# Three split operations moved to GpSimd, the first experts' output added in two halves, one expert result per state early in the scan

## The reference

```
h = layernorm(x) * (1 + ca) + sa
x = x + ga * attention(h)              # 8 heads, latent keys and values, causal softmax
h = layernorm(x) * (1 + cb) + sb
x = x + gb * experts0(h)               # 8 experts of 64 hidden units, top 2 of 8, gelu
h = layernorm(x) * (1 + ca1) + sa1
x = x + ga1 * mixer(h)                 # state-space layer, below
h = layernorm(x) * (1 + cb1) + sb1
x = x + gb1 * experts1(h)              # 8 experts of 512 hidden units, top 2 of 8, gelu

mixer: x_in, res = h @ in_w + in_b     # 256 channels each
       xc = silu(conv4(x_in))
       d_raw, B, C = xc @ x_proj_w + x_proj_b      # 16 columns each
       delta = softplus(d_raw @ dt_w + dt_b)
       for each token: state = exp(delta * A) * state + delta * xc * B ; y = sum_n state_n * C_n
       out = ((y + xc * D) * silu(res)) @ out_w + out_b
```

## Time and profile before

| | |
|---|---|
| median of 3 runs | 1304.76 us (1299.76 to 1305.74) |
| the profiled execution | 1305.41 us, span of its instructions 1303.6 us |
| VectorE busy | 1014.4 us, 78% of the span |
| TensorE busy | 1040.4 us, 80% |
| ScalarE busy | 751.6 us, 58% |
| GpSimd busy | 632.4 us, 49% |
| mean granted TensorE clock | 0.909 of full speed |

### The profile page before, as it was taken

How to read it: one execution, slowest core, us unless ns; L and a number is a source line. 1 busy time by engine, 2 the same in 40 slices (tenths; PEclk the granted TensorE clock), 3 DMA queues, 4 the chain that set the end, 5 groups by cost and what they waited for, 6 DMA issues and landing times. The chain is left out here.

```text
span 1303.6 us, 19636 instructions
## 1 busy us (share of the span) xinstructions
PE 1040.4 (80%) x6224; PEld 702.5 (54%) x6224; DVE 1014.4 (78%) x2221; ACT 751.6 (58%) x1483; POOL 632.4 (49%) x446
## 2 busy tenths in 40 slices
PE   5894679887997889887988889878988788877191
PEld 4551136555655556565665555555655565655181
DVE  3766988689788988799888988799888977699301
ACT  2544446478647766577647765576647764575030
POOL 0102952179334963188335952197335942098402
PEclk8896569989998999989998999989998998989596
DMA  5201202262143503261144403271145404061451
GB/s 165 74 9 58 81 0 90 80 219 81 31 153 134 174 25 128 56 240 60 32 152 163 146 29 133 64 234 49 48 136 188 128 23 144 31 232 54 157 164 45
DMA packets 74151, 137.24 MB, mean 105 GB/s; under 512 B 10504, under 2 KB 44344, under 8 KB 73920
## 3 DMA queue, kind: packets, MB, share of 16 engines
q1 hardware_dynamic: 67936, 123.20, 28.5%
q0 software_dynamic: 5392, 12.59, 3.0%
q10 hardware_dynamic: 720, 0.19, 0.1%
HBM read 116.34 MB, written 15.42 MB: 101 GB/s over the span
## 5 line engine op out<-in xcount | busy, mean ns | idle before, releaser
L1692 DVE TENSOR_TENSOR_SCAN probs_T<-bank,probs_T 128x512 f32<-128x512 f32 x256 | 299.4, 1209 | 8.7 <-ACT bank L1245 7.0
L598 POOL TENSOR_TENSOR probs_T<-step_space,probs_T 128x1024 f32<-128x1024 f32 x112 | 263.8, 2361 | 3.1 <-DVE probs_T L1692 3.1
L1245 ACT ACTIVATE bank<-step_space,a_neg 128x512 f32<-128x512 f32 x256 | 169.5, 685 | 69.8 <-DVE probs_T L1692 65.0
L1170 ACT ACTIVATE probs<-bank,row_neg 128x128 f32<-128x128 f32 (+3 forms) x256 | 135.2, 530 | 125.2 <-DVE row_neg L1555 107.8
L880 PE MATMUL bank<-k_pad,q_lat 128*128 128x512 f32 (+3 forms) x512 | 188.0, 454 | 3.1 <-DMA k_pad<-xc 3.1
L1555 DVE TENSOR_REDUCE row_neg<-bank 128x1 f32<-128x128 f32 (+3 forms) x256 | 122.6, 486 | 82.0 <-PE bank L882 79.9
L617 POOL TENSOR_TENSOR step_space<-step_space,probs 128x512 f32<-128x512 f32 x112 | 142.2, 1269 | 44.1 <-DVE probs L1349 43.8
L844 PE MATMUL bank<-probs,w_ident 128*128 128x512 f32 x256 | 154.0, 687 | 8.1 <-DVE probs L1349 8.1
L1349 DVE TENSOR_TENSOR probs<-probs_T,bank 128x1024 f32<-128x1024 f32 x128 | 153.4, 1199 | 5.5 <-PE bank L1030 3.8
L1030 PE MATMUL bank<-split,select 96*128 96x512 bf16 x128 | 55.8, 436 | 111.8 <-DVE probs L1349 85.1
L791 PE MATMUL bank<-expert_w,hidden 128*128 128x128 f32 x960 | 144.3, 298 | 0.0
(11 more groups left out here) (214 smaller groups left out, 1856.8 us busy)
## 6 DMA issues: line engine op xcount, KB each, us to landing
expert_w<-in_experts_dram SPq DMA_DIRECT2D x120, 512.0 KB, 5.1
probs_T<-b_rows_dram SPq DMA_DIRECT2D x64, 512.0 KB, 4.2
slots_in<-slots_dram SPq DMA_DIRECT2D x24, 256.0 KB, 3.3
results_dram<-slots_out SPq DMA_DIRECT2D x24, 256.0 KB, 4.3
k_pad<-xc SPq DMA_DIRECT2D x64, 64.0 KB, 2.0
x_in<-in_x_dram POOLq DMA_DIRECT2D x8, 256.0 KB, 3.3
gate<-gate_rows_dram SPq DMA_DIRECT2D x1, 2048.0 KB, 7.1
out_dram<-x_out POOLq DMA_DIRECT2D x7, 256.0 KB, 3.6
```

Of the source, the lines that this page charges most:

```text
L598: ins = nc.gpsimd.tensor_tensor(inject[:, n % 3, :, :], u[:], row.unsqueeze(1).to_broadcast([P, DH, T]), ALU.mult)
L1170: f(probs_ring[:, n % 4, 0:(i + 1) * P], bank[SCORE_BANK[n % 4]][:, 0:(i + 1) * P], ACT.Exp, bias=row_neg[:, n % 4:n % 4 + 1], accum_out=r ...
L1245: f(decay(k)[:], delta[:, c, :], ACT.Exp, scale=a_neg[:, c, n:n + 1]).then_inc(dec_ok.sem, 1)
L1692: v.tensor_tensor_scan(state[:, n % 2, c, :], decay(DH * n + c)[:], inject[:, n % 3, c, :], 0.0, ALU.mult, ALU.add).then_inc(st_ok.sem, 1)
```

## The change

GpSimd does the low part's three operations in a new function, `split_last`, ahead of its first inject. It starts when VectorE's middle part is done (`split_mid`), and each operation waits for the one before. The output of the small experts goes to two banks, tiles 0 and 1 to bank 6, tiles 2 and 3 to bank 1, so that VectorE adds and takes statistics in two halves; TensorE waits for bank 1's keys to be copied before, and for both halves before it projects the next keys into bank 1. In the tables, block 3's result is moved from state 0 to ahead of the scan, the quad (fill 8) from state 1 to 0, block 5's result from state 1 to 3, and ScalarE copies the quad after decay 4 in place of 6.

```diff
+        EARLY_OUT = (OUT_BANK, 1)
-        out0_mm = signal("out0_mm", 1)
-        out0_add = signal("out0_add", 1)
+        out0_mm = signal("out0_mm", 2)
+        out0_add = signal("out0_add", 2)
+            def split_last(b):
+                low = slice(2 * L, 3 * L)
+                pool.wait_ge(*(gated_weight(b + 1, BIAS) if b < B - 1 else gated_weight(b, OUT)))
+                pool.wait_ge(split_mid.sem, split_mid.at(b, 1))
+                nc.gpsimd.tensor_tensor(part[low, :], proj[low, :], split[low, :], ALU.subtract).then_inc(split_low.sem, 1)
+                pool.wait_ge(split_low.sem, split_low.at(b, 1))
+                nc.gpsimd.tensor_copy(split[low, :], part[low, :]).then_inc(split_low.sem, 1)
+                pool.wait_ge(split_low.sem, split_low.at(b, 2))
+                nc.gpsimd.tensor_tensor(split[low, :], part[low, :], split[low, :], ALU.subtract).then_inc(split_ok.sem, 1)
             def sum_states(b):
+                split_last(b)
+                pool.wait_ge(split_ok.sem, split_ok.at(b, 1))
                 for n in range(2):
...
-                    pool.wait_ge(out0_mm.sem, out0_mm.at(b, 1))
+                    pool.wait_ge(out0_mm.sem, out0_mm.at(b, 2))
                     gate_proj(b + 1)
...
                     for t in range(NT):
-                        ins = mm(bank[OUT_BANK][:, t * P:(t + 1) * P], gated[:, c, t * P:(t + 1) * P],
-                                 gated_proj[:, c, :], start=(c == 0 and t == 0), stop=(c == C0 - 1), skip_group_check=True)
-                    return ins
+                        ins = mm(bank[EARLY_OUT[t // 2]][:, t * P:(t + 1) * P], gated[:, c, t * P:(t + 1) * P],
+                                 gated_proj[:, c, :], start=(c == 0 and t % 2 == 0), stop=(c == C0 - 1),
+                                 skip_group_check=True)
+                        if c == C0 - 1 and t % 2 == 1:
+                            ins.then_inc(out0_mm.sem, 1)
...
+                if ahead:
+                    pe.wait_ge(k_lat.sem, k_lat.at(b + 1, 1))
                 out0(0)
...
                 if ahead:
+                    pe.wait_ge(out0_add.sem, out0_add.at(b, 2))
                     project(b + 1, 3)
...
                 if behind:
-                    pe.wait_ge(out0_add.sem, out0_add.at(b, 1))
+                    pe.wait_ge(out0_add.sem, out0_add.at(b, 2))
                 early(2)
...
-                dve.wait_ge(out0_mm.sem, out0_mm.at(b, 1))
-                tt(x[:], x[:], bank[OUT_BANK][:].rearrange("p (t d) -> p t d", d=P), ALU.add).then_inc(out0_add.sem, 1)
-                dve.wait_ge(out0_add.sem, out0_add.at(b, 1))
-                ln_stats(b, 2, x, link)
+                for half in range(2):
+                    dve.wait_ge(out0_mm.sem, out0_mm.at(b, half + 1))
+                    tiles = slice(2 * half, 2 * half + 2)
+                    source = bank[EARLY_OUT[half]][:, 2 * half * P:(2 * half + 2) * P].rearrange("p (t d) -> p t d", d=P)
+                    tt(x[:, tiles, :], x[:, tiles, :], source, ALU.add).then_inc(out0_add.sem, 1)
+                    dve.wait_ge(out0_add.sem, out0_add.at(b, half + 1))
+                    ins = ln_half_stats(half, x)
+                link(ins)
+                ln_aggregate(link)
...
                 link(cp(split[:], proj[0:3 * BC, :]))
-                mark(tt(split[mid, :], proj[mid, :], split[mid, :], ALU.subtract))
+                tt(split[mid, :], proj[mid, :], split[mid, :], ALU.subtract).then_inc(split_mid.sem, 1)
                 clip_dt(0)
                 clip_dt(1)
-                mark(tt(part[low, :], proj[low, :], split[low, :], ALU.subtract))
...
-                        if c == 0 and n == 0:
-                            dve.wait_ge(chain.sem, chain.at(b, CHAIN["main"] - 1))
-                            link(cp(split[low, :], part[low, :]))
-                            tt(split[low, :], part[low, :], split[low, :], ALU.subtract).then_inc(split_ok.sem, 1)
...
-            _done(0) + _fills(6, 7) + _done(1) + _fills(7, 8) + _done(2))
-PE_SCAN = {0: _done(3), 1: _fills(8, 9) + _done(4, 5), 2: _fills(9, 11), 4: _done(6) + _fills(11, 12),
+            _done(0) + _fills(6, 7) + _done(1) + _fills(7, 8) + _done(2, 3))
+PE_SCAN = {0: _fills(8, 9), 1: _done(4), 2: _fills(9, 11), 3: _done(5), 4: _done(6) + _fills(11, 12),
...
-ACT_SCAN = {2: _fills(6, 8), 3: [("results", 0)], 6: _fills(8, 9), 8: _fills(9, 11), 14: _fills(11, 13),
+ACT_SCAN = {2: _fills(6, 8), 3: [("results", 0)], 4: _fills(8, 9), 8: _fills(9, 11), 14: _fills(11, 13),
```

More of the change, by code:

```diff
@@ L326, in build @@
         pr_out = signal("pr_out", 1)
+        split_mid = signal("split_mid", 1)
+        split_low = signal("split_low", 2)
         split_ok = signal("split_ok", 1)
@@ L990, in main @@
                 for c in range(1, C0):
-                    ins = out0(c)
-                ins.then_inc(out0_mm.sem, 1)
+                    out0(c)
                 early(0)
@@ L1379, in ln_aggregate @@
                 link(ins)
[L1381 to L1384, removed]
             def ln_normalise(b, j, x, mark, link):
@@ L1668, in iteration @@
                 dve.wait_ge(pr_out.sem, pr_out.at(b, 1))
-                mid, low = slice(L, 2 * L), slice(2 * L, 3 * L)
+                mid = slice(L, 2 * L)
                 link(cp(split[:], proj[0:3 * BC, :]))
-                mark(tt(split[mid, :], proj[mid, :], split[mid, :], ALU.subtract))
+                tt(split[mid, :], proj[mid, :], split[mid, :], ALU.subtract).then_inc(split_mid.sem, 1)
                 clip_dt(0)
                 clip_dt(1)
-                mark(tt(part[low, :], proj[low, :], split[low, :], ALU.subtract))
                 for c in range(DH):
@@ L1740, in _ @@
                    ).then_inc(last_half, 1)
-CHAIN = {"tail": 2, "attend": 15, "main": 30, "head": 19, "act main": 2}
+CHAIN = {"tail": 2, "attend": 15, "main": 27, "head": 19, "act main": 2}
 CONV_ORDER = ((0, 0), (0, 1), (1, 0), (2, 0), (1, 1), (3, 0), (2, 1), (3, 1))
```

## The result

The changed kernel took 1285.82 us in the median of four runs (1281.85 to 1286.94) and the kernel before, over its four runs, 1302.26. The ratio is 0.9868, with a 95% interval of 0.9830 to 0.9906: 1.3% faster, 17 us by the ratio. Forecast was faster by 13 us, to 1292, within 1287 to 1301. The sign was right, and the time came out 1.2 us under the range. Two later measurements of the same kernel gave 0.9841 (0.9804 to 0.9878) and 0.9880 (0.9840 to 0.9919).

A forecast was written before the change was run, and what follows sets the result against it. The prediction took VectorE to bound the scan, with GpSimd the next limit at the third read product. Its terms, 2.9 + 2.2 + 7.0 + 1.0 = 13.1 us off 1305.41, gave about 1292 as median, range 1287 to 1301.

The forecast's parts named there:

- What bounds it: In the scan VectorE is busiest, GpSimd nearly as busy; GpSimd's first addition would then hold the third read product 1 to 2 us.
- the rival of 1276: In the scan VectorE gets all 2.83 us a batch back, 28.6 us in all; chance 0.04.
- the signs: Listed trace evidence: among it, scan stage about 1.5 us shorter, in batches 2, 4 and 7 over 2.5.
- GpSimd's three operations: Two subtractions and a copy moved off VectorE before the scan's injects: GpSimd's first addition 0.36 us earlier a batch, 2.9 us.
- S: Time from the middle subtraction's end to the end of GpSimd's three operations, forecast at 3.74 us.
- The C row's term: Early in the scan, reordered expert results end VectorE's waits for TensorE's C row at the third read product: 2.2 us.
- The prediction's short cut: VectorE's C row waits, 3.8 us in total, less the 0.4 GpSimd would take in each of the four anyway.
- The decays: In the scan, earlier fills and quad copy make decay 9 ready in time; all 7.0 us of VectorE's waiting goes.
- The rival of the low clock: TensorE idles before state 1, its clock stays low through both fills, decay 9 stays late: gain 6, 1298.5; chance 0.13.
- The halves: Addition of the first experts, ahead of the scan, done in two halves started earlier: 0.12 us a batch, 1.0 us.
- The slow rival: GpSimd is slow at its three operations and becomes the bound: slower than before, 1320 at the upper bound; chance 0.07.
- cheap operations on GpSimd: Rival: GpSimd's three operations take 0.45 to 0.8 us each, its first addition ends 0.8 earlier: 16.6 less, 1288; chance 0.16.

The follow-up runs named there:

- The order alone: The kernel before with only the three tables of expert results changed; the split operations stay on VectorE and the addition is not halved: ratio 0.9979 (0.9949 to 1.0009).
- the last run: The changed kernel with the quad (fill 8) back in state 1 on TensorE and after decay 6 on ScalarE: ratio 0.9849 (0.9801 to 0.9897).
- the run with three more subtractions: The changed kernel with GpSimd's first low-part subtraction done four times in each batch, output the same: ratio 1.0016 (0.9988 to 1.0044) against the kernel before.
- the run with one more subtraction: The changed kernel with GpSimd's first low-part subtraction done twice in each batch, output the same: ratio 0.9894 (0.9862 to 0.9925) against the kernel before.
- the addition first: The changed kernel with GpSimd's first addition of read products ahead of its inject for state 4: ratios 0.9835, 0.9852 and 0.9820 against the kernel before.

## Why the prediction was right in kind and short in size

**What bounds it: right.** The forecast that GpSimd's addition takes over as the limit of the third read product, in every batch, for 1 to 2 us, held: 1.4 us, eight times. So did what follows from it, that VectorE doesn't get its 2.1 us a batch back (the rival of 1276). The scan stage shortened as the signs had it, by 1.2 to 2.0 us in batches 1, 3, 5 and 6 and by 2.8 to 3.4 in batches 2, 4 and 7.

**GpSimd's three operations: the step that failed**, by size. The prediction put S at 3.74 us, let the last operation hold the first u to its end, and started the injects 0.3 us later than before. S was 3.2 (the copy 0.60 and not 0.9, the subtractions 1.15 and not 1.27), u was held 0.12 us, and GpSimd then still waited for the B rows, 0.82 us in batch 4. The injects started where they had started before, within 0.3 us either way, on average 0.1 us later in batches 1 to 7 over the three traces. The 0.7 us back from the three injects was right, 4.43 to 3.71. Counted from the middle subtraction's start, GpSimd's first addition ended 0.71 us earlier in the mean of batches 1 to 7 (0.64 in the third trace), where the term had 0.36, and 1.5 us earlier in batch 0, where the first inject waited for the first u and not for rows. That is 6.5 us in place of 2.9, the largest part by far of what the sum was short. This term and the next one together were forecast at 5.1 and measured 9.6.

**The C row's term: right in kind, wrong in its owner.** The prediction charged 2.2 us to the order of the results. In the whole change it is 3.1: so much later than GpSimd's limit (the addition's end and 0.2 us) did the third read product come before, in batches 2, 4, 5 and 7. The prediction's short cut, VectorE's idle time less 0.4 us, gives the right size in three of them (0.9, 0.1 and 0.8) and fails in batch 2, where VectorE itself was 0.6 us behind GpSimd's limit and the whole delay was 1.3 us, not 0.3. The order alone also yields 3.1, of which 0.5 is chance, the first inject having started up to 0.34 us sooner in that trace. And GpSimd's operations alone do the same: TensorE, given the split early, no longer idles ahead of C row 0, and its granted clock up to the third read product is 0.91 to 1.00.

**The decays: right.** 7.0 forecast, 7.2 to 7.6 measured over the three traces, by the mechanism given (fills earlier, table change no longer late); only the quad's part in it was wrong, the last run shows. The rival of the low clock did come about in part: TensorE idled 2.30 us ahead of state 1 and block 4's result took 1.84 us, but the clock was back for the fills, 1.05 us for the second, and ScalarE waited 0.37 us in place of 2.38. That it would be back was a bet in the prediction on one row of 3.85 us, and luck has a share in it:

```profile
697.80 0.39 PE L1050 MATMUL bank<-split,select 96*128 96x512 bf16 x1 [2.30 <-DVE probs L1369]
...
698.95 1.84 PE L807 MATMUL bank<-expert_w,hidden 128*128 128x128 f32 x8
...
704.33 1.05 PE L792 MATMUL bank<-slots_T,expert_w 128*128 128x128 f32 x8
```

```profile
705.42 0.60 ACT L1103 ACTIVATE hidden<-bank 128x512 f32<-128x512 f32 x1 [0.37 <-PE bank L792]
```

**The halves:** 1.0 forecast, 1.9 measured. The start is 0.44 us earlier, near the 0.47 reckoned; the two additions cost 0.20 more than one and not 0.33. (0.47 less 0.33 is 0.14 and not the 0.12 written, 1.1 us in all.)

**The slow rival** had its threshold at S = 5.4, three operations of 1.7 us. By the run with three more subtractions the gain is used up only at S = 7.6, since there was more gain to use up, and since up to 4.8 the operations lie mostly in slack, which the prediction's straight line had not.

**The range.** Its lower end came from cheap operations on GpSimd (1288), which is the case that came nearest to the truth by its effect, GpSimd's addition 0.7 to 0.8 us earlier, and not by its cause: the subtractions took 1.15 us and not 0.45 to 0.8, and it was the slack up to the first inject that covered them. That the C row's term and the halves could be short as well was not in it. A smaller misreading did no harm: that GpSimd's 128x512 rows hardly vary doesn't hold for its scaling of weights, 1.72 us in the mean for that size.

## What to carry to other kernels

Moving work from a busy engine to a half-idle one pays by what the receiving engine's next deadline allows, so find the instruction that will wait for it and count the slack up to it; here it was one addition, and an inject put behind it was worth another 10 us up to there, of which 7.6 were left at the scan's end and about 4 in the runs' time. When a stall ends on an engine that had been idling, look at what made that engine late before reordering its work: feeding TensorE earlier removed the same 3 us as the reordering did, with the granted clock at 0.91 or more. And judge sub-percent parts of such a pipeline by stretches of the trace, since their sums over seven batches agree to 0.5 us between traces of the changed kernel where whole runs differ by 10; then look in the stretches outside for what is paid back.

## What the hardware did that I had not expected

- GpSimd's subtraction on 32 partitions takes 1.15 us and an operation of two inputs on 128 partitions 1.27 (2.36 with twice the elements), so the time goes by elements per partition. Both subtractions read one 16-bit operand, which at 1.15 cost nothing that shows, and a 16-bit output made no difference (1.16). Its copy of 512 elements takes 0.60, about half (0.68 from start to start). The Trainium skill ("GPSIMD Engine Reference", Performance versus the Vector engine) has 769 ns for a tight one-input loop of that length; the trace has less, and decides.
- The lock between VectorE and GpSimd works in both directions, by who came first: the first u held for 0.12 us in the changed kernel by a GpSimd operation, and in the run with one more subtraction GpSimd's operation held by u, 1.49 for 1.16. The Trainium skill ("SBUF — State Buffer", Who interferes with whom) says that issue order decides who blocks; the traces agree. For the split operations I had weighed only one of the two directions.
- TensorE's clock is not a matter of the last gap alone. After 2.69 us of waiting, ahead of 695.83 in the run with GpSimd's operations alone, the granted clock was 1.00, the level of 2.4 GHz; after 2.30 us ahead of 697.80 in the changed kernel eight matmuls soon took 1.84 us for 1.11, and the granted clock from 697.80 to 702.00 was 0.66.
- The clock also falls in one batch and not in another, at identical work. The stretch from attention's first addition to the small experts' takes 17.3 us in six of the changed kernel's batches, and 19.6 in batch 6. By stretch, in this order, batch 6 whole, batch 5 whole, and a part of batch 6:

```profile
936.24:955.81 19.57, 17.79 (x81) 11.53 (x81) 14.44 (x52) 5.83 (x10) 2.77 (x2) 0.83 0.31 97
794.03:811.30 17.27, 15.21 (x81) 9.58 (x81) 14.37 (x52) 5.83 (x10) 2.78 (x3) 1.00 0.35 110
...
941.00:946.00 5.00, 4.76 (x15) 3.41 (x16) 3.42 (x8) 1.37 (x2) 2.77 (x2) 0.55 0.50 142
```

  The fall begins behind a wait of 1.03 us that every batch has. It hit batch 6 in the first trace of the changed kernel, batches 4 and 6 in the second, and none of batches 0 to 6 in the third; in the run with the order alone it hit two:

```profile
515.71:535.93 20.22, 18.47 (x86) 12.00 (x85) 14.45 (x53) 5.83 (x10) 2.77 (x2) 0.83 0.31 94
```

  It cost 2.3 to 2.5 us each in the changed kernel and with the order alone, and 1.1 to 3.9 with the addition first. Whether it is chance stays open, and there is a sign against it: in the four traces with the old order of results it hit none of 28 batches, and in the ten traces with the new order 12 of 70, 2.8 us an execution. So the new order may provoke it and pay back part of its gain; no run tests this. Some executions also have their first attention done 6 us earlier (its first addition at 73 in place of 79 us; both occur with the addition first). The two together are of the size of the spread between runs of one kernel, which is argued from the traces, since the other executions have none. What sets either off stays open.
